# A four-layer conditioned sequence kernel on one core: the last two pairs' state products moved to VectorE, the last projection and gathering cut into parts, and new tables for the order of all engines

## The reference, cut to what matters

```python
B, T, D, DI, N = 8, 512, 256, 512, 16        # float32
x = linear_attention(x, cond, mask0, heads=16)   # layer 0
x = mamba(x, cond)                               # layer 1
x = mamba(x[:, order], cond), back in order      # layer 2
x = linear_attention(x, cond, mask3, heads=8)    # layer 3

# linear_attention: xn = layernorm(x); q, k, v = xn @ W + b
#   q = softmax over a head's width, k = softmax over tokens
#   y = q @ (k^T v), per head
#   h = silu(layernorm(y) * (1 + scale(cond)) + shift(cond)) @ Wo + bo ; x + h
# mamba: h = modulated layernorm(x); xm, z = h @ W_in
#   xm = silu(causal_conv4(xm)); dt_r, Bm, Cm = xm @ W_x; dt = softplus(dt_r @ W_dt + b)
for t in range(T):                               # for each of 512 channels and 16 states
    h = h * exp(dt[t] * A) + (dt[t] * xm[t]) * Bm[t]
    y[t] = sum over states of h * Cm[t]
#   y = (y + xm * D_param) * silu(z); x + gate(cond) * (y @ W_out)
```

## Time and profile before

| | us |
|---|---|
| median of 3 runs | 2083.55 |
| lowest and highest | 2068.17 and 2085.44 |
| the profiled execution | 2081.06 |
| its span, first to last instruction | 2079.2 |
| first work of POOL for a scan (L915) starts at | 124.38 |
| last product of POOL (L949) ends at | 2008.21 |

### The profile page before, as it was taken

The page is one execution under the profiler, slowest core; times in us unless marked ns, Lnnn a source line. Parts: engine busy times, 40 slices in busy tenths (PEclk is TensorE's granted clock), DMA queues, the critical chain, the costliest instruction groups (busy, mean ns, idle before and its releaser), DMA issues. The chain is left out here.

```text
span 2079.2 us, 29187 instructions
## 1 busy us (share of the span) xinstructions
PE 1841.1 (89%) x9282; PEld 1286.2 (62%) x9282; DVE 1781.6 (86%) x1816; ACT 1735.6 (83%) x3242; POOL 1795.5 (86%) x825
## 2 busy tenths in 40 slices
PE   9877798998999999899989989899999989797788
PEld 7545565657666565667667565666667566556566
DVE  5457989998998998899998988999998998898963
ACT  2389888899989899999989889999989898876642
POOL 0058999999998999999998989999998999999960
PEclk9898899999999999999999999999999999897799
DMA  7034444454444544445444535354444544444420
GB/s 271 1 95 148 158 164 156 135 168 152 147 141 150 169 139 162 145 152 173 151 148 145 173 124 181 130 164 164 152 146 147 179 137 148 146 152 154 157 68 21
DMA packets 163785, 302.30 MB, mean 145 GB/s; under 512 B 18904, under 2 KB 27312, under 8 KB 162096
## 3 DMA queue, kind: packets, MB, share of 16 engines
q1 hardware_dynamic: 153110, 287.45, 42.1%
q10 hardware_dynamic: 10522, 12.99, 2.0%
HBM read 292.98 MB, written 5.29 MB: 143 GB/s over the span
## 5 line engine op out<-in xcount | busy, mean ns | idle before, releaser
L949 POOL TENSOR_TENSOR state<-state,c_rows 128x1024 f32<-128x1024 f32 x512 | 1199.6, 2366 | 43.1 <-DVE state L1555 35.5
L1555 DVE TENSOR_TENSOR_SCAN state<-decay,mix_banks 128x512 f32<-128x512 f32 x576 | 674.2, 1207 | 26.5 <-ACT decay L1277 8.3
L1915 PE MATMUL bank<-const_sb,state 128*128 128x128 f32 x4096 | 552.1, 284 | 94.1 <-POOL state L949 93.6
L1915 PEld LDWEIGHTS bank<-const_sb,state 128*128 128x128 f32 x4096 | 485.5, 146 | 204.1 <-POOL state L949 126.2
L940 POOL TENSOR_TENSOR state<-kept,b_rows 128x1024 f32<-128x1024 f32 x224 | 529.9, 2367 | 41.8 <-PE bank L1915 19.6
L1552 DVE TENSOR_TENSOR_SCAN state<-mix_banks,state 128x512 f32<-128x512 f32 x448 | 525.7, 1203 | 45.3 <-ACT mix_banks L1260 33.3
L1277 ACT ACTIVATE decay<-kept,ssm_pack 128x512 f32<-128x512 f32 x576 | 394.5, 715 | 10.8 <-DVE state L1555 7.1
L1545 DVE TENSOR_TENSOR mix_banks<-kept,mix_banks 128x1024 f32<-128x1024 f32 x288 | 353.5, 1228 | 45.7 <-ACT mix_banks L1268 24.1
L1260 ACT ACTIVATE mix_banks<-kept,ssm_pack 128x512 f32<-128x512 f32 x448 | 305.0, 684 | 85.8 <-DVE state L1555 78.9
L967 ACT ACT_TABLE_LOAD x183 | 234.8, 1283 | 37.2 <-DVE prep_minus L1397 17.7
L1797 PE MATMUL bank<-kept,conv_diag 128*128 128x512 f32 x496 | 225.8, 596 | 4.5 <-ACT kept L1204 4.2
(11 more groups left out here) (201 smaller groups left out, 2253.9 us busy)
## 6 DMA issues: line engine op xcount, KB each, us to landing
b_rows<-flat_rows SPq DMA_DIRECT2D x512, 256.0 KB, 3.8
c_rows<-flat_rows SPq DMA_DIRECT2D x512, 256.0 KB, 3.5
conv_diag<-conv_diag SPq DMA_DIRECT2D x8, 1024.0 KB, 7.4
out<-x_res ACTq DMA_DIRECT2D x8, 512.0 KB, 3.2
ssm_pack<-ssm_pack SPq DMA_DIRECT2D x2, 1907.0 KB, 12.2
x_next<-x ACTq DMA_DIRECT2D x6, 512.0 KB, 5.2
x_again<-x_dbl ACTq DMA_DIRECT2D x16, 128.0 KB, 2.4
state<-ada_w SPq DMA_DIRECT2D x1, 1536.0 KB, 13.8
```

The costliest lines, as they stand in the source:

```text
L949: pool.tensor_tensor(st, st, by_pair(c_rows[:, row % ROWS]), ALU.mult).then_inc(m_prod, 1)
L1555: ins = dve.tensor_tensor_scan(st, decay[:, nth(g) % DECAYS], mixed, 0.0, ALU.mult, ALU.add)
L1915: ins = pe.matmul(y_banks[c2][:, t * P:(t + 1) * P], state[:, g % STATES, t * P:(t + 1) * P], ident, start=False, stop=(g == BANK_SUMS[g / ...
```

## The change

1. `LATE_PAIRS = 2`: the products of the last two pairs (units 1020 to 1023) are taken from POOL's `weight` and made by DVE in `weight_late`, right after the last unit's scan. `sum_up` waits for their own semaphore.
2. In the last scan alone, PE multiplies the first two gated chunks by their weights at two places, early0 and early1, ahead of the last gate, into the same two banks that out0 and out1 then finish with the other two chunks. The chunks y2 and y3 are turned in the y banks.
3. In the last scan alone, the gathering's first half begins with the two token tiles that come from out0, before out1's copy is waited for.
4. `KINDS`, the bases, all stage tables, `STEPS`, `GATES`, `SKIPS` and the numbers of fillers are new. On ACT the row has 165 table loads in place of 183; PE's row has 98 filler matmuls in place of 113. All other instructions are the same in number, but for DVE's inputs (L1545), of which 144 in place of 128 go to banks that do not lie in ascending order side by side.

```diff
-KINDS = (SPREAD, BESIDE, SPREAD, SPREAD, BESIDE, SPREAD, BESIDE, SPREAD, BESIDE, SPREAD, BESIDE, SPREAD, SPREAD, BESIDE, SPREAD, BESIDE)
-FIRST_BASES = {'att': (-60, -28), 'setup': -50, 'prep': -50}
-TAIL_BASE, POST_BASE, PREP_BASE = -7, -46, 9
-ATT_BASES, LATE_BASES = (10, 100, 159, 222), (41, 207)
+KINDS = (SPREAD, BESIDE, SPREAD, SPREAD, BESIDE, SPREAD, BESIDE, SPREAD, BESIDE, SPREAD, SPREAD, BESIDE, BESIDE, SPREAD, SPREAD, BESIDE)
+FIRST_BASES = {'att': (-53, -28), 'setup': -49, 'prep': -33}
+TAIL_BASE, POST_BASE, PREP_BASE = -19, -50, 8
+ATT_BASES, LATE_BASES = (18, 100, 153, 222), (41, 193)
+LATE_PAIRS = 2
...
 POST_STAGES
-    8: (181, 181, 183, 182, 183, 198, 198, 200, 202, 201, 203, 207, 215, 220, 221, 222, 222, 222, 222, 222, 222),
+    8: (201, 201, 210, 213, 214, 215, 217, 216, 216, 216, 218, 218, 220, 222, 228, 234, 237, 240, 240, 240, 240,
+        240, 240),
...
-FILLERS = {(0, 'turn0'): 18, (0, 'k0'): 20, (0, 'yT0'): 16, (15, 'turn0'): 26, (15, 'k0'): 0, (15, 'yT0'): 23, (15, 'out0'): 0}
-PREP_FILLERS = 10
+FILLERS = {(0, 'turn0'): 23, (0, 'k0'): 4, (0, 'yT0'): 9, (15, 'turn0'): 18, (15, 'k0'): 0, (15, 'yT0'): 19, (15, 'out0'): 12}
+PREP_FILLERS = 13
...
-    "weight": range(0, ALL_UNITS, HC),
+    "weight": range(0, ALL_UNITS - HC * LATE_PAIRS, HC),
...
+            def weight_late(k):
+                g = ALL_UNITS - HC * (LATE_PAIRS - k)
+                ...
+                dve.wait_ge(c_loaded[row % ROWS], 16 * (si * (HALVES * N // ROWS) + row // ROWS + 1))
+                dve.wait_ge(m_scan, g + HC)
+                st = pair_states(g)
+                dve.tensor_tensor(st, st, by_pair(c_rows[:, row % ROWS]), ALU.mult).then_inc(m_late, 1)
...
                 if part == PARTS // 2 and is_unit(g):
                     scan(g)
+                    if g == ALL_UNITS - 1:
+                        for k in range(LATE_PAIRS):
+                            weight_late(k)
...
+                if qi + 1 == SCANS:
+                    yield from w.to("early0")
...
+                    banks = [free(post_fill(qi, f"out{h}")) for h in range(2)]
+                    early = in_two_parts(banks, u[s], gated_w[:], range(HC), False)
+                    next(early)
+                    yield from w.to("early1")
+                    all_of(early)
+                    for c in range(HC, CH):
+                        yield from turn_gated(c)
+                    yield from w.to("out0")
...
+                    late = in_two_parts(banks, u[s], gated_w[:], range(HC, CH), True)
...
+                    gathered(first, 0, range(0, 2))
+                    yield from w.to("gather0+")
+                    taken(pe, post_fill(qi, "out1"))
+                    gathered(first, 0, range(2, TT)).then_inc(first_full, 1)
+                    yield from w.to("gather1")
+                    second, second_full = free(post_fill(qi, "gather1"))
+                    gathered(second, 1, range(TT)).then_inc(second_full, 1)
```

More of the change, by code:

```diff
@@ L1242, in after @@
                     yield from w.to(f"take{c}")
[L1243 removed]
+                    if qi + 1 == SCANS and c >= HC:
+                        act.wait_ge(l_full[c - HC], 1)
+                        bank_, done = y_banks[c - HC], l_taken[c - HC]
+                    else:
+                        bank_, done = filled(act, post_fill(qi, f"y{c}"))
                     act.activation(u[s][:, c, :], bank_[:], ACT.Copy).then_inc(done, 1)
```

139 lines of the change are left out of this document (105 added, 34 removed), and 443 rows, old and new, of tables (ATT_STAGES, POST_STAGES, PREP_STAGES, STEPS).

## The result

The changed kernel takes 2012.22 us (median of 4 runs, 2009.57 to 2021.50), the kernel before 2079.45 beside it (4 runs, 2068.17 to 2085.44): a ratio of 0.9686, interval [0.9653, 0.9718]. The profiled execution is the slowest of the four (2021.50, span 2019.3); a second profile, taken later, has a span of 2011.4. In the traces each float32 matmul of the program stands as two, so 16 in the order are x32 in a row.

A forecast was written before the change was run, and what follows sets the result against it. Three stages were seen: opening, stream (four engines 89 to 95% busy, POOL nearest to full), and a PE, DVE and ACT chain behind it. From 2081.06, -9 - 8 - 4.4 - 11.5 = -32.9 gave 2048 us; range 2026 to 2068.

The forecast's parts named there:

- I take 40% of DVE's 20 us, -8 us: Stream: later residuals save DVE about 20 us of waits, of which 40% reach POOL: -8 us.
- the order is much better: Rival, in the stream: the new order gains 30 us there, total 2026 us; chance 0.12.
- The bound -30: Stream: the most the new order may gain, at most half of POOL's 59 us of waits.
- The opening (-9): Before the stream: PE work taken out ahead of the first attention's output projection, less what comes back later: -9 us.
- 8.7 us come back: Opening: layer 2's gates, layer 3's products and turned keys return in the preparation, 8.7 us, 1 given to short pauses.
- the opening only shifts PE's work: Part of the rival that the stream gives all back: opening gains 0, only the end's parts hold, 2065 us; chance 0.19.
- The last products (-4.4): Stream's end: POOL loses two products to DVE and its last one ends 4.65 us earlier: -4.4 us.
- DVE ends 0.2 us after POOL: Last products: after POOL's last input, two scans and two late products bring DVE's end 0.2 us behind POOL's.
- a lock: Rival, last products: DVE's late products and POOL block each other, 2.2 us, total 2050; held for 0.5 within the forecast's case.
- The end (-11.5): Behind the last product: half projection early, gathering's pause gone, norm and table load earlier, fillers added: -11.5 us.
- Conditions named as wrong: Profile signs against the forecast: first L915 after 121 us, DVE's bank waits above 60, POOL idle above 100 in the stream.
- POOL idle near 80: Sign expected in the profile after: POOL's idle time in the stream near 80 us instead of 91.9.

The follow-up runs named there:

- res_late: Kernel before with the residual later in DVE's row, three quarters of a unit in layer 1 and two in layer 2: 0.9985 of before.
- order_alone: Code of the kernel before with all numbers (places, leads, bases, fillers) of the changed kernel, without its three code edits: 0.9745 of before, median 2024.97 us.
- open_fill: Changed kernel with the opening's filler matmuls of the kernel before (18, 20, 16 and 10 in place of 23, 4, 9 and 13): 0.9715 of before.
- after_supply_b: A run that the study names only here; the text given tells neither its change nor its time.
- the two with cut sums: Kernel before with ACT's eight sums of each attention's second norm, or first norm, reading 32 of 256 columns: 0.9981 and 0.9987 of before.
- res_early: Changed kernel with the residual as close behind PE's last half projection as in the kernel before: 0.9757 of before, median 2026.43 us.
- opening_alone: Kernel before with only the opening's bases, stage-table rows and fillers of the changed kernel: 1.0028 of before.
- edits_alone: Changed kernel's code (late products, early half projection, gathering in parts) with all places and numbers of the kernel before: 0.9985 of before.
- states16_after: Changed kernel with 16 state buffers in place of 14: 0.9676 of before.

## Why the prediction was wrong

**The order's worth in the stream (the step "I take 40% of DVE's 20 us, -8 us"): wrong, by 22 us.** It went -30.4, the size that I had given 12 in 100 as "the order is much better"; with the other three parts the time fell below that rival's 2026, too. Two parts of the step failed. The saving at each residual was worked out as if all else stayed in time; res_late shows that in the old order 3 quarters take 11.1 us from these waits, not 20, and give 7.5 to the next one. And the whole was taken from the one cause that I could price. order_alone shows that the numbers alone do it; none of the five runs that moved the residual, the norm or the buffers in the kernel before brought more than 5 us by the medians. The bound -30 was half of the waits in the earlier trace rows, and the stream came out at it; what was wrong was to stay so near to zero within it. That -30 fits is luck as much as judgment: no run ties it to half of those waits.

**The opening (-9): mis-sized, -16.2 and -18.8 in two profiles.** Its first part held: the projection ends at 57.99, 58 forecast. So did the second: the pause behind it, 6.38 us before (74.65 to 81.04), still ends 6.39 behind it (64.38), with layer 1's gates and layer 2's products in it. The step that failed is "8.7 us come back", less 1. From the preparation's first rows to POOL's first work it took 43.34 us before and 43.77 after, +0.4 instead of +7.7, although layer 2's gates, layer 3's products and turned keys are now in it. PE alone in the two stretches (us, busy, granted clock), before and then changed:

```profile
81.04:124.38 43.34, 39.05 (x113) 0.93 0.14 36
```
```profile
64.38:108.15 43.77, 43.71 (x159) 0.93 0.02 5
```

PE's pauses gave 4.2 us (4.29 idle before, 0.06 after), of which I had counted 1. Its work grew by 4.7 us and not by 8.7. Layer 2's gates are an example. Before, they took 3.58 us, nearly all of it between 60 and 70 us, with a granted clock of 0.67. In their new place,

```profile
90.50 1.89 PE L1639 MATMUL mix_banks<-kept,silu_c 128*8 128x256 f32 x8
```

they take 1.89 us, and from 90 to 100 us the granted clock is 1.00. The rows, before and then changed, 60 to 90 us in tens:

```profile
60.00:70.00 10.00, 10.00 (x47) 6.63 (x46) 2.35 (x11) 0.00 (x0) 0.00 (x0) 0.67 0.00 0
70.00:80.00 10.00, 4.65 (x13) 2.73 (x11) 5.91 (x25) 2.02 (x5) 0.21 (x1) 0.67 0.00 0
80.00:90.00 10.00, 8.49 (x24) 5.00 (x24) 4.60 (x11) 2.78 (x5) 0.20 (x1) 0.65 0.00 1
```
```profile
60.00:70.00 10.00, 9.04 (x54) 7.37 (x54) 8.14 (x31) 3.49 (x8) 0.40 (x2) 0.83 0.00 1
70.00:80.00 10.00, 10.00 (x25) 3.88 (x24) 8.05 (x17) 3.19 (x7) 0.00 (x0) 1.00 0.01 2
80.00:90.00 10.00, 10.00 (x32) 5.52 (x30) 2.51 (x5) 5.83 (x7) 0.00 (x0) 1.00 0.00 0
```

Before, PE was granted mostly 1.2 GHz from 60 to 90 us, behind the gates and the condition's small products and across the pause; after, it is busy without a break from 70 to 100 us and has 2.4 GHz. I had priced items at the lower level and a fall of the clock as a risk on the slow side, and never asked what a rise would give. By the profiles on record the clock is the smaller part, though. Over all runs but open_fill, after_supply_b and the two with cut sums, seven profiles with the opening of before have POOL's first work at 120.4 to 125.8 us, 123.8 on average, and nine with that of the changed kernel at 104.9 to 111.1, 106.9 on average: -17. At the same mean clock up to there, 0.88, it is 123.8 to 125.8 us against 111.1 (res_early), still some 13 us. The fillers don't explain it (110.2 in open_fill). And opening_alone shows that early first step sizes by themselves are lost again: for them the rival "the opening only shifts PE's work" was right.

**The last products (-4.4): mis-sized, -1.5.** The step "DVE ends 0.2 us after POOL" failed: it ends 3.1 after. POOL's input for the last pair is done at 1952.35, as I had placed it, but DVE then has another pair's scans and half of attention 14's result to do and begins the last pair's scans at 1955.51, 1.5 us before POOL's last product ends. DVE is the later one, a case that stood among the bounds and not in the sum. The duration of a late product was right, 2.33 / 2 = 1.16 us (1.23 taken), and a lock cannot be seen in the changed kernel, since POOL is done 0.8 us before the first one starts.

**The end (-11.5): right, -11.8.** Norm statistics follow the last residual at once (1975.18 against 1974.35 + 0.69), the gathering has no pause before it, no table load stands on the chain. ACT's second turned half ends at 2008.99 and the fillers at 2010.62, so they cost the 1.6 us that were forecast; the kernel without them was not run. edits_alone adds a condition that I had not seen: in the old order the edits shorten the time behind the last product by 1.05 us (71.0 to 69.95), in the new one by 4.5 (63.7 to 59.2).

**Conditions named as wrong.** None came: first work before 121 us, DVE's waits for decays in banks at 33.3 us (57.4 with those for the B rows), POOL idle below 100. "POOL idle near 80" became 62.7, "residual waits about halved" became a seventh.

**What stays open.** Why the new order loses 30 us and more less in the stream. In the kernel before, neither the residual's place nor the number of state buffers nor ACT's work at one place gives more than 5 us by the medians; whether another single wait would was not tried. Undoing the residual's place costs some 12 us of it. The rest was not isolated; the leads of the decays alone were not varied.

## What to carry to other kernels

Where engines run in a fixed order and wait for each other in turn, the wait at the head of a row is where the lateness shows, not what it costs: try the single move before pricing it, and expect the next wait to take its place. A new order as a whole can be worth several times what the one wait that can be priced in it gives, and a part of it put into another order can cost far more than the whole gains, so its range has to be wide on both sides. For a part that starts earlier, ask what the second thing of its kind needs. And take several profiles before reading a few microseconds from one: here the same opening differs by 6 us and the same stream by 8.

## What the runs showed of the hardware

Two executions of the changed kernel differ by 2.6 us at POOL's first work (108.15 and 105.56), and their granted clock with them: from 40 to 50 us PE is busy 10.00 of 10 us in both, at 0.66 in the one and 1.00 in the other. Over nine profiles with this opening it goes from 104.89 us at a mean granted clock of 0.95 up to there (states16_after) to 111.06 at 0.88 (res_early).

The pair of late products, 128x1024 each with both operands in SBUF, takes DVE 2.33 us; POOL takes 2.38 for one.
